# Polymax attention on VectorE: two instructions, add and multiply, replaced by one scalar_tensor_tensor

## The chip, the cores and the metric

The kernel runs on all 8 cores of one Trainium2 chip. Every core executes the same program on its own data: a pair of cores shares one of the four sequences, and each core of a pair owns 16 of the 32 query tiles of 128 rows. There is no traffic between cores. The time is the device time of the slowest core, in microseconds (us).

## The reference

One pre-norm layer over x of shape (4, 4096, 1024), in float32, with 16 heads of 64. In place of softmax the attention uses a polynomial, and masked scores count as zero after it:

```python
def polymax(x):                      # X_INT=-100, Y_INT=1, POWER=2, DIVISOR=1000
    lin  = where((x >= -100) & (x <= 0), -0.01 * x + 1, 0)
    poly = where(x > 0, x ** 2 + 1, 0)
    return (poly + lin) / 1000
...
att = polymax(where(causal, q @ k.T / 8, -inf))
x = x + (att @ v) @ W_proj                       # on layernorm(x)
x = x + gelu((layernorm(x) @ U1) @ V1 + b1) @ U2 @ V2 + b2
```

For a score s between -100 and anything positive, 1000 * polymax(s) = 1 - 0.01 s + r (r + 0.01) with r = max(s, 0). The kernel computes the term r (r + 0.01) tile by tile; the linear term 1 - 0.01 s needs no elementwise work on tiles that are wholly visible, since its sum over keys is a running product of k and v, kept in `msnap` and `prefsnap`.

## The kernel before, in words

The program is written engine by engine: `b.op` appends an instruction to an engine's queue and has it raise that engine's counter, and `b.wait` appends a wait for a counter to the queue, so each engine works through its queue strictly in order. The order in which the Python emits is the order of the work.

The stages are: LayerNorm of x; the K, V and Q projections (lines 616 to 663); attention on the first 2048 keys (`half` 0); the K and V projections of the other 2048 keys (lines 918 to 950); attention on those (`half` 1); the output projection (line 1047); the second LayerNorm and the low-rank FFN.

`emit_attention(half)` runs over four query chunks c of 512 columns and, within each, over 8 pairs p of heads. Such a (c, p) block goes through key tiles of 128 keys: 8 masked ones for c = 0, 8 full ones and 8 masked ones for c = 1, 16 full ones for c = 2 and 3, all in half 0; 8 masked for c = 2, and 8 full and 8 masked for c = 3, in half 1. A tile holds 128 keys by 2 heads by N queries; N is 512 in a full tile, and 512, 512, 384, 384, 256, 256, 128, 128 in the masked ones of a block. So there are 48 blocks and 640 tiles: 384 full, 256 masked, and by size 448 of 1024 elements in each partition (2 x 512) and 64 each of 768, 512 and 256.

A tile idx passes through three engines:

- TensorE: two QK matmuls (line 735) into a pair of PSUM banks. `emit_qk(idx + 3)` stands in its queue ahead of `emit_av(idx)`.
- ScalarE: `relu` of the scores into `eb` (line 756), and on masked tiles also 1 - 0.01 s of the diagonal 128 columns into `zb` (line 761).
- VectorE: `eb + 0.01` into `ab2` (line 770), then `ab2 * eb` into `gb` (line 777); on masked tiles `zb` times the mask (line 783) and `gb` times the mask (line 788), over 128 of the columns.
- TensorE: two AV matmuls (line 810) with `gb`, and on masked tiles two more with the masked `zb` (line 818); the first tile of a block also adds the `msnap` products (line 836).

Buffers `eb` and `gb` and the score banks are rings of three tiles (`sb = idx % 3`), `ab2` one of two. `s_rel` tells that ScalarE has read a score bank, `e_rel` that VectorE has finished with the `eb` slot, `g_rel` that TensorE has finished with the `gb` slot. At the end of a block VectorE copies the result out of PSUM (lines 883 to 895), and TensorE starts the next block's QK only after the last AV.

On VectorE the multiplication of line 777 waits for VectorE's own counter (`b.wait("vector", "V", acnt)`): it reads what line 770 has just written.

Of the kernel before, what the change touches and what calls it, by code (L numbers as in the profile page):

```python
# [11 lines left out]
ALU = mybir.AluOpType  # L12
# [112 lines left out]
def view(pool, byte_off, dtype, shape):  # L125
    esz = mybir.dt.size(dtype)
    assert byte_off % 32 == 0 and byte_off % esz == 0
    n = prod(shape[1:])
    ap = pool.bitcast(dtype).ap()[0:shape[0], byte_off // esz: byte_off // esz + n]
    if len(shape) > 2:  # L130
        names = [f"a{i}" for i in range(len(shape) - 1)]
        spec = "p (" + " ".join(names) + ") -> p " + " ".join(names)
        ap = ap.rearrange(spec, **{names[i]: shape[i + 1] for i in range(len(shape) - 1)})
    return ap


def build_program(upto="full", dumps=()):
# [27 lines left out]
    with contextlib.ExitStack() as stack:  # L165
# [19 lines left out]
        b = Build(nc)  # L185
# [8 lines left out]
        def tfence():  # L194
# [31 lines left out]
        eb = view(poolD, 0, BF16, [128, 6, 512])  # L226
# [11 lines left out]
        ab2 = [view(poolD, 14336, BF16, [128, 2, 512]),  # L238
               view(poolD, 16384, BF16, [128, 2, 512])]
# [24 lines left out]
        def bank(i, lo=0, hi=512):  # L264
            return ps[:, i * 512 + lo: i * 512 + hi]
# [140 lines left out]
        for tb in range(8):  # L406
# [28 lines left out]
            for dc in range(DC):  # L435
                if dc + 2 < DC:
# [9 lines left out]
                     inc="T")  # L446
# [21 lines left out]
        for tb in range(8):  # L468
# [26 lines left out]
            for dc in range(DC):  # L495
                if dc + 2 < DC:
# [3 lines left out]
                                 o=lnxh[tb // 4][:, dc, (tb % 4) * 512:(tb % 4 + 1) * 512],  # L500
                                 t=tmp2[dc % 4], n=bank(bkb): e.tensor_add(o, t, n),
                                 inc="V")
# [188 lines left out]
        def emit_attention(half):  # L691
# [6 lines left out]
            for c in range(4):  # L698
# [3 lines left out]
                for p in range(NP):  # L702
# [5 lines left out]
                    if K_ILV and half == 0 and tb2 == 0:  # L708
# [8 lines left out]
                                         inc="V")  # L717
# [21 lines left out]
                    def is_m(idx):  # L739
                        return 8 * c <= kts[idx] <= 8 * c + 7  # L740

                    gcnt, mcnt, pcnt = {}, {}, {}

                    def emit_eg(idx, qkT):
                        ktg = kts[idx]
                        sb = idx % 3
                        masked = is_m(idx)
                        j0 = max(4 * c + 1, ktg // 2 + 1)
                        coloff = (j0 - (4 * c + 1)) * 128
                        N = 512 - coloff  # L750
                        b.wait("scalar", "T", qkT)
                        b.wait("scalar", "V", e_rel[sb])
                        b.wait("scalar", "P", e_relP[sb])
                        b.op("scalar", lambda e, o=eb[:, 2 * sb:2 * sb + 2, 0:N],
                             i=ps8[:, SBK[sb]:SBK[sb] + 2, 0:N]:
                             e.activation(o, i, AF.Relu), inc="S")  # L756
                        if masked:
                            b.wait("scalar", "V", zw_rel[sb])
                            b.op("scalar", lambda e, o=zb[:, sb, :, :],
                                 i=ps8[:, SBK[sb]:SBK[sb] + 2, 0:128]:  # L760
                                 e.activation(o, i, AF.Identity, scale=-0.01,  # L761
                                              bias=consts[:, 1:2]), inc="S")
                        s_rel[sb] = b.cnt["S"]
                        b.wait("vector", "S", s_rel[sb])
                        if idx >= 2:
                            b.wait("vector", "V", gcnt[idx - 2])
                        acnt = b.op("vector",
                                    lambda e, o=ab2[idx % 2][:, :, 0:N],
                                    i=eb[:, 2 * sb:2 * sb + 2, 0:N]:
                                    e.tensor_scalar_add(o, i, 0.01), inc="V")  # L770
                        b.wait("vector", "T", g_rel[sb])
                        b.wait("vector", "V", acnt)
                        gcnt[idx] = b.op("vector",
                                         lambda e, o=gb[:, 2 * sb:2 * sb + 2, 0:N],
                                         a=ab2[idx % 2][:, :, 0:N],
                                         i=eb[:, 2 * sb:2 * sb + 2, 0:N]:
                                         e.tensor_mul(o, a, i), inc="V")  # L777
                        pcnt[idx] = 0
                        if masked:
                            midx = ktg % 2  # L780
                            zw_rel[sb] = b.op("vector", lambda e, o=zmb[:, sb, :, :],
                                              z=zb[:, sb, :, :], m=masksb[:, midx, :, :]:
                                              e.tensor_mul(o, z, m), inc="V")  # L783
                            b.wait("vector", "V", gcnt[idx])
                            mcnt[idx] = b.op("vector",
                                             lambda e, o=gb[:, 2 * sb:2 * sb + 2, 0:128],
                                             m=masksb[:, midx, :, :]:
                                             e.tensor_mul(o, o, m), inc="V")  # L788
                        e_rel[sb] = b.cnt["V"]
# [56 lines left out]
                    for idx in range(nk):  # L846
                        emit_eg(idx, fences[idx])
                        if idx + 3 < nk:
                            fences[idx + 3] = emit_qk(idx + 3)
                        emit_av(idx)  # L850
                        if K_ILV and half == 0 and idx < 8:
                            b.wait("tensor", "V", kcast[hc])
                            if idx == 0:
                                b.wait("tensor", "V", av_free[idle_bk])
                                b.wait("tensor", "S", av_freeS[idle_bk])
                            b.op("tensor", lambda e, o=bank(idle_bk),
                                 l=wkvh[hc % 2][:, idx, :],
                                 r=lnxh[1][:, idx, tb2 * 512:(tb2 + 1) * 512],
                                 st=(idx == 0), sp=(idx == 7):
                                 e.matmul(o, l, r, skip_group_check=True, start=st,  # L860
                                          stop=sp), inc="T")
# [16 lines left out]
                    for i4 in range(4):  # L878
# [3 lines left out]
                        if not chunk_final:  # L882
                            b.op("vector", lambda e, o=dst, s=src: e.tensor_copy(o, s),
                                 inc="V")
                        elif c <= 1:
                            if j == 1:
                                b.op("vector", lambda e, o=dst, s=src: e.tensor_copy(o, s),
                                     inc="V")
# [4 lines left out]
                        else:  # L893
                            b.op("vector", lambda e, o=dst, s=src, pv=prefsnap[:, j, p:p + 1]:
                                 e.scalar_tensor_tensor(o, s, pv, o, ALU.add, ALU.add),
                                 inc="V")
# [218 lines left out]
        for c in range(4):  # L1115
# [32 lines left out]
            for fc in range(32):  # L1148
# [3 lines left out]
                                      i=bank(2 + fc % 2), bb=b1s[:, fc:fc + 1]:  # L1152
# [136 lines left out]
```

How the kernel before makes its waits and increments, by code:

```python
        def wrapped(e, fn=fn, h=h, w=selfw):  # L60
            i = fn(e)
            if w:
                i.wait_op(h, w, "sem-ge")
            i.then_inc(h, 1)
# [3 lines left out]
    def _dma_on(self, queue, dst, src, slot=None):  # L68
        key = f"dma{self.dma_n}"
        self.dma_n += 1
        if not hasattr(self, "dma_slots"):
            self.dma_slots = {}
        if slot is None:
            slot = key
        if slot not in self.dma_slots:
            assert len(self.dma_slots) < self.N_DMA_SEMS, "DMA sem pool exhausted"
            self.dma_slots[slot] = [self.dma_sems[len(self.dma_slots)], 0]
        ent = self.dma_slots[slot]
        ent[1] += 16
        h = ent[0]
        self.sem_handles[key] = h
        self.cnt[key] = ent[1]
        for e_ in self.ENGINES:
            self.last_wait[e_][key] = 0
        self.streams[queue].append(
            lambda e, d=dst, s=src, h=h: e.dma_start(out=d, in_=s).then_inc(h, 16))
        return key
# [7 lines left out]
    def wait(self, eng, sem, val):  # L95
        if not val or val <= 0:
            return
        if sem.startswith("dma"):
            val = self.cnt[sem]
        assert val <= self.cnt[sem], f"{eng} waits future {sem}={val} (now {self.cnt[sem]})"
        if self.last_wait[eng][sem] >= val:
            return
        self.last_wait[eng][sem] = val
        h = self.sem_handles[sem]
        self.streams[eng].append(lambda e, h=h, v=val: e.wait_ge(h, v))
```

## Time and profile before

| | |
|---|---|
| median of 8 runs | 2139.38 us (2132.04 to 2173.7) |
| the profiled execution's own time | 2140.15 us |
| its span on the slowest core (core 7) | 2138.6 us |
| the other cores' spans | 2118.0 to 2137.8 us |
| mean granted TensorE clock, by core | 0.721 to 0.729 |
| busy on core 7: TensorE, VectorE, ScalarE | 1295.6, 1215.0, 760.7 us |
| lines 770 and 777 together on VectorE | 635.4 us in 1280 instructions |

The span runs from the first to the last instruction; 1.55 us of the execution's time lie outside of it. Busy times add up the durations of instructions, and neighbours on one engine can overlap by some tens of ns, so an engine's cost per tile is read from the starts of its instructions and not from their durations. The attention stages lie at about 518 to 1120 us and 1386 to 1650 us of the span.

### The profile page before, as it was taken

To read this page: it belongs to the slowest core of one execution; us is meant where nothing else is said; L and a number is where in the kernel's file an instruction comes from. 1 tells how busy PE (TensorE), PEld (TensorE's weight loads), DVE (VectorE), ACT (ScalarE), POOL (GpSimd) and SP (SyncE) were. 2 spreads that over 40 slices of the span, in tenths; PEclk is the share of its full clock that TensorE was granted. 3 is DMA by queue.
4 is the path that set the end of the run, shared out by engine and by line. 5 is a ranking of instruction groups with operands and counts; after the bars stand their busy time and mean duration, and the time that the engine had idled before them with its cause. 6 is when DMAs were issued, how large, how long until landed. Compare 5 with 4: busy or idle time off the path is not lost.

```text
span 2138.6 us, 23901 instructions; the slowest of 8 cores (2118.0 to 2138.6 us)
## 1 busy us (share of the span) xinstructions
PE 1295.6 (61%) x6880; PEld 469.6 (22%) x6880; DVE 1215.0 (57%) x2811; ACT 760.7 (36%) x1074; POOL 0.2 (0%) x4
## 2 busy tenths in 40 slices
PE   3423286477667676766662837666765461368886
PEld 0001133243222221111111313322221130023332
DVE  4558433245788888888882323488887233344422
ACT  1200000002667777778770000266775000133332
POOL 0000000000000000000000000000000000000000
PEclk8755597798556668777885969855665685578997
DMA  5445201200000000000002020000000444001011
GB/s 162 157 129 185 79 30 49 79 1 1 1 1 1 1 1 1 1 1 1 1 1 79 13 66 1 1 1 1 1 1 16 153 145 120 0 0 40 40 40 40
DMA packets 37408, 87.76 MB, mean 41 GB/s; under 512 B 1953, under 2 KB 7330, under 8 KB 37282
## 3 DMA queue, kind: packets, MB, share of 16 engines
q1 hardware_dynamic: 30562, 75.75, 10.9%
q10 hardware_dynamic: 6720, 10.49, 1.6%
q8 instruction: 60, 0.98, 0.2%
q14 instruction: 66, 0.54, 0.1%
HBM read 77.85 MB, written 8.39 MB: 40 GB/s over the span
## 4 chain that ended last, share of the span: by engine, by line
PE 45%; DVE 27%; issue 12%; DMA 10%; ACT 4%; DVEq 1%; SPq 0%; ACTq 0%
DVE poolD L777 9%; PE ps L810 8%; DVE poolD L770 6%; DMA poolD<-W_attn 6%; PE ps L735 5%; PE ps L1141 3%; PE ps L946 3%; PE ps L636 3%; PE ps L1047 3%; PE ps L931 3%; PE ps L616 3%; PE ps L658 3%; PE ps L1161 3%; ACT poolD L756 2%; DMA poolD<-W_proj 1%
## 5 line engine op out<-in xcount | busy, mean ns | idle before, releaser
L756 ACT ACTIVATE poolD<-ps 128x1024 bf16<-128x1024 f32 (+3 forms) x640 | 560.9, 901 | 882.2 <-PE ps L735 666.2
L810 PE MATMUL ps<-poolD,poolA 128*64 128x512 bf16 (+3 forms) x1280 | 308.6, 467 | 255.1 <-DVE poolD L777 120.1
L777 DVE TENSOR_TENSOR poolD<-poolD 128x1024 bf16<-128x1024 bf16 (+3 forms) x640 | 391.9, 612 | 68.2 <-DVE poolD L770 2.2
L735 PE MATMUL ps<-poolB,poolA 64*128 64x512 bf16 (+3 forms) x1280 | 285.5, 473 | 33.8 <-ACT poolD L761 16.4
L770 DVE TENSOR_SCALAR poolD<-poolD 128x1024 bf16<-128x1024 bf16 (+3 forms) x640 | 243.5, 380 | 44.3 <-ACT poolD L756 23.2
L810 PEld LDWEIGHTS ps<-poolD,poolA 128*64 128x64 bf16 x1280 | 93.8, 119 | 446.1 <-issue 446.1
L1153 ACT ACTIVATE poolC<-ps,sb_b1s 128x512 bf16<-128x512 f32 x128 | 88.0, 688 | 117.7 <-PE ps L1141 76.8
L761 ACT ACTIVATE poolD<-ps,consts 128x256 bf16<-128x256 f32 x256 | 124.3, 485 | 0.0
L735 PEld LDWEIGHTS ps<-poolB,poolA 64*128 64x128 bf16 x1280 | 65.0, 102 | 237.2 <-issue 236.0
L818 PE MATMUL ps<-poolD,poolA 128*64 128x128 bf16 x512 | 86.6, 306 | 0.0
L946 PE MATMUL ps<-poolD,poolC 128*128 128x512 bf16 x256 | 62.9, 402 | 37.5 <-DVE poolD L918 37.5
L616 PE MATMUL ps<-poolC,poolD 128*128 128x512 bf16 x256 | 57.6, 389 | 41.9 <-DVE poolD L595 41.9
L1047 PE MATMUL ps<-poolC,poolD 128*128 128x512 bf16 x256 | 57.9, 391 | 40.4 <-DVE poolD L989 40.4
L1141 PE MATMUL ps<-poolC,poolB 128*128 128x512 bf16 x256 | 78.8, 393 | 5.4 <-DVE poolC L1126 1.5
L931 PE MATMUL ps<-poolC,poolD 128*128 128x512 bf16 x256 | 57.8, 390 | 38.2 <-DVE poolD L918 38.2
L384 ACT ACTIVATE poolD<-ps 1x512 f32<-1x512 f32 x4 | 2.3, 587 | 216.8 <-PE ps L380 216.8
L658 PE MATMUL ps<-poolC,poolD 128*128 128x512 bf16 x256 | 61.2, 392 | 28.0 <-DVE poolD L595 27.2
L1161 PE MATMUL ps<-poolC,poolB 128*128 128x512 bf16 x256 | 76.7, 382 | 1.5 <-ACT poolC L1153 1.3
L378 PE MATMUL ps<-poolD,sb_onescol 128*1 128x512 bf16 x32 | 18.9, 590 | 95.9 <-DVE poolD L375 95.9
L443 PE MATMUL ps<-poolD,sb_onescol 128*1 128x512 bf16 x64 | 33.0, 515 | 70.1 <-DVE poolD L440 69.9
L636 PE MATMUL ps<-poolD,poolC 128*128 128x512 bf16 x256 | 58.1, 392 | 26.7 <-DVE poolD L595 26.7
L788 DVE TENSOR_TENSOR poolD<-poolD,sb_masksb 128x256 bf16<-128x256 bf16 x256 | 72.7, 284 | 0.3 <-DVE poolD L783 0.3
(101 smaller groups left out, 1224.9 us busy)
## 6 DMA issues: line engine op xcount, KB each, us to landing
poolD<-x_t SPq DMA_DIRECT2D x8, 2048.0 KB, 9.9
poolA<-x_t SPq DMA_DIRECT2D x8, 2048.0 KB, 10.2
poolD<-W_attn SPq DMA_DIRECT2D x12, 1024.0 KB, 5.0
poolD<-W_attn SPq DMA_DIRECT2D x16, 512.0 KB, 3.6
poolC<-x_own_t SPq DMA_DIRECT2D x8, 1024.0 KB, 6.1
y<-poolC SPq DMA_DIRECT2D x4, 2048.0 KB, 6.8
poolD<-W_proj SPq DMA_DIRECT2D x8, 512.0 KB, 3.7
poolD<-U ACTq DMA_DIRECT2D x5, 512.0 KB, 4.8
```

The source lines that it names most:

```text
L636: sp=(dc == DC - 1): e.matmul(o, l, r, skip_group_check=True, start=st, stop=sp), inc="T")
L658: e.matmul(o, l, r, skip_group_check=True, start=st, stop=sp), inc="T")
L735: e.matmul(o, l, r, skip_group_check=True, start=True, stop=True, tile_position=tp),
L756: e.activation(o, i, AF.Relu), inc="S")
L761: e.activation(o, i, AF.Identity, scale=-0.01, bias=consts[:, 1:2]), inc="S")
L770: e.tensor_scalar_add(o, i, 0.01), inc="V")
L777: e.tensor_mul(o, a, i), inc="V")
L810: e.matmul(o, l, r, skip_group_check=True, start=st, stop=True, tile_position=tp),
L946: e.matmul(o, l, r, skip_group_check=True, start=st, stop=sp), inc="T")
L1047: e.matmul(o, l, r, skip_group_check=True, start=st, stop=sp), inc="T")
L1141: e.matmul(o, l, r, skip_group_check=True, start=st, stop=sp), inc="T")
L1161: e.matmul(o, l, r, skip_group_check=True, start=st, stop=sp), inc="T")
```

## The change

The addition into `ab2` and the multiplication that reads it become one `scalar_tensor_tensor`, which computes (eb + 0.01) * eb straight into `gb`. With it go the buffer `ab2`, VectorE's wait for its own addition, and the wait for the multiplication of two tiles earlier. The waits for ScalarE and for the `gb` slot stay.

```diff
                         b.wait("vector", "S", s_rel[sb])
-                        if idx >= 2:
-                            b.wait("vector", "V", gcnt[idx - 2])
-                        acnt = b.op("vector",
-                                    lambda e, o=ab2[idx % 2][:, :, 0:N],
-                                    i=eb[:, 2 * sb:2 * sb + 2, 0:N]:
-                                    e.tensor_scalar_add(o, i, 0.01), inc="V")
                         b.wait("vector", "T", g_rel[sb])
-                        b.wait("vector", "V", acnt)
                         gcnt[idx] = b.op("vector",
                                          lambda e, o=gb[:, 2 * sb:2 * sb + 2, 0:N],
-                                         a=ab2[idx % 2][:, :, 0:N],
                                          i=eb[:, 2 * sb:2 * sb + 2, 0:N]:
-                                         e.tensor_mul(o, a, i), inc="V")
+                                         e.scalar_tensor_tensor(o, i, 0.01, i,
+                                                                ALU.add, ALU.mult),
+                                         inc="V")
```

## Rows read from the trace of the kernel before

**Rows 1.** The page: busy time of the engines, and VectorE in 40 slices (tenths).
```profile
PE 1295.6 (61%) x6880; PEld 469.6 (22%) x6880; DVE 1215.0 (57%) x2811; ACT 760.7 (36%) x1074; POOL 0.2 (0%) x4
DVE  4558433245788888888882323488887233344422
```

**Rows 2.** The two attention stages by windows: stretch, its length, engines' busy us, PEclk, DMA.
```profile
518.00:1120.00 602.00, 409.78 (x2164) 122.38 (x2160) 503.85 (x1268) 445.33 (x574) 0.00 (x0) 0.70 0.00 1
1386.00:1650.00 264.00, 175.80 (x1080) 57.53 (x1076) 221.07 (x670) 185.07 (x304) 0.00 (x0) 0.59 0.00 1
```

**Rows 3.** Waits, 819 to 1120 us: who for whom, us in total, times, longest.
```profile
PE ps L810 <- DVE poolD L777: 84.3, 171, 0.7
DVE poolD L770 <- ACT poolD L756: 11.9, 14, 0.9
```

**Rows 4.** Timeline of VectorE, full tiles: start, duration (us), engine, line, operation.
```profile
962.97 0.42 DVE L770 TENSOR_SCALAR poolD<-poolD 128x1024 bf16<-128x1024 bf16 x1
963.49 0.69 DVE L777 TENSOR_TENSOR poolD<-poolD 128x1024 bf16<-128x1024 bf16 x1
964.10 0.42 DVE L770 TENSOR_SCALAR poolD<-poolD 128x1024 bf16<-128x1024 bf16 x1
...
978.83 0.42 DVE L770 TENSOR_SCALAR poolD<-poolD 128x1024 bf16<-128x1024 bf16 x1
```

**Rows 5.** Timeline of VectorE in one masked block (tiles of 768, 512 and 256).
```profile
613.11 0.35 DVE L770 TENSOR_SCALAR poolD<-poolD 128x768 bf16<-128x768 bf16 x1
613.57 0.56 DVE L777 TENSOR_TENSOR poolD<-poolD 128x768 bf16<-128x768 bf16 x1
614.04 0.28 DVE L783 TENSOR_TENSOR poolD<-poolD,sb_masksb 128x256 bf16<-128x256 bf16 x1
...
614.45 0.35 DVE L770 TENSOR_SCALAR poolD<-poolD 128x768 bf16<-128x768 bf16 x1
...
615.78 0.29 DVE L770 TENSOR_SCALAR poolD<-poolD 128x512 bf16<-128x512 bf16 x1
...
618.05 0.22 DVE L770 TENSOR_SCALAR poolD<-poolD 128x256 bf16<-128x256 bf16 x1
...
618.59 0.28 DVE L783 TENSOR_TENSOR poolD<-poolD,sb_masksb 128x256 bf16<-128x256 bf16 x1
...
618.99 0.22 DVE L770 TENSOR_SCALAR poolD<-poolD 128x256 bf16<-128x256 bf16 x1
```

**Rows 6.** Groups of VectorE by form: count, busy us, mean ns, idle before.
```profile
L777 DVE TENSOR_TENSOR poolD<-poolD 128x1024 bf16<-128x1024 bf16 x448 | 310.3, 693 | 47.6 <-DVE poolD L770 1.4
L770 DVE TENSOR_SCALAR poolD<-poolD 128x1024 bf16<-128x1024 bf16 x448 | 188.5, 421 | 43.6 <-ACT poolD L756 23.2 <-ACT poolD L761 20.0 <-issue 0.2
...
L777 DVE TENSOR_TENSOR poolD<-poolD 128x256 bf16<-128x256 bf16 x64 | 18.7, 292 | 6.8 <-DVE poolD L770 0.4
...
L895 DVE SCALAR_TENSOR_TENSOR poolC<-ps,prefsnap,poolC 128x128 bf16<-128x128 f32 x64 | 18.0, 344 | 10.9 <-PE ps L818 10.9
...
L464 DVE SCALAR_TENSOR_TENSOR poolB<-poolD,poolB 1x512 f32<-1x512 f32 x8 | 5.4, 679 | 12.7 <-ACT poolB L461 12.7
L454 DVE TENSOR_TENSOR poolB<-poolD 1x512 f32<-1x512 f32 x8 | 5.4, 679 | 20.0 <-ACT poolD L452 20.0
```

**Rows 7.** Timeline of VectorE: two groups of four evacuations, each group back to back.
```profile
960.08 0.89 DVE L883 CAST poolC<-ps 128x128 bf16<-128x128 f32 x4 [0.89 <-PE ps L810]
...
1562.56 1.13 DVE L895 SCALAR_TENSOR_TENSOR poolC<-ps,prefsnap,poolC 128x128 bf16<-128x128 f32 x4 [0.68 <-PE ps L818]
```

**Rows 8.** Timeline of ScalarE: masked tiles of 256, then four full tiles together.
```profile
615.96 0.39 ACT L756 ACTIVATE poolD<-ps 128x256 bf16<-128x256 f32 x1 [0.37 <-DVE poolD L788]
616.24 0.47 ACT L761 ACTIVATE poolD<-ps,consts 128x256 bf16<-128x256 f32 x1
...
621.30 3.77 ACT L756 ACTIVATE poolD<-ps 128x1024 bf16<-128x1024 f32 x4 [3.46 <-DVE poolC L892]
```

**Rows 9.** Timeline of TensorE: one AV matmul pair of a masked tile.
```profile
616.01 0.53 PE L810 MATMUL ps<-poolD,poolA 128*64 128x384 bf16 x2 [0.48 <-DVE poolD L788]
```

## The prediction

> **What bounds the kernel now.** I read the page first. Its totals name no bound (TensorE 61% busy, VectorE 57%), but the row of slices does: VectorE stands at 7 to 8 tenths in the slices of the two attention stages and at 2 to 5 in most others [rows 1]. The windows of those two stages, 866 us together, give VectorE 724.9 us, ScalarE 630.4 us, TensorE 585.6 us of busy time [rows 2]. The chain of waits inside them says who is late: in the stretch of full tiles the AV matmuls wait 84.3 us for the multiplication of line 777, while VectorE's addition waits for ScalarE only 14 times, once at the head of each block, 11.9 us in all [rows 3]. So inside a block VectorE is the bound, and ScalarE and TensorE run ahead of it and are held by the rings of three tiles.
>
> Because VectorE is the bound, what matters is the distance between the starts of its instructions. The timeline of full tiles shows it bare: additions at 962.97 and 978.83 with 13 more between them, so 14 tiles in 15.86 us, 1.133 us a tile, of which 0.525 lies between addition and multiplication and 0.61 between multiplication and next addition [rows 4]. The reader should see that these are not the durations (421 and 693 ns, [rows 6]): the next addition starts 80 ns before the multiplication has ended, whereas the multiplication starts some 105 ns after the end of the addition, for whose result it waits.
>
> In a masked block the same is read by size. The two mask products take 614.04 to 614.45 or 618.59 to 618.99, 0.405 us a tile. Two tiles of 768 take 613.11 to 615.78, two of 512 take 615.78 to 618.05, one of 256 takes 618.05 to 618.99 [rows 5]. Less the masks, addition and multiplication together take 0.93 us, 0.73 us and 0.535 us.
>
> **The change part by part.** *Removed: the addition with the wait behind it.* By the starts it holds VectorE for 0.525 us of a 1024 tile [rows 4] and 0.46 us of a 768 tile [rows 5]. The other dropped wait, for the multiplication two tiles back, was over long before and costs nothing now.
>
> *Put in place of the multiplication: one scalar_tensor_tensor, bf16 in and out of SBUF.* The trace has no such row, so its cost has two ends. The multiplication's duration falls from 693 ns at 1024 elements to 292 ns at 256, that is 0.522 ns an element [rows 6]; its spacing of 0.61 us [rows 4] is then 0.075 us plus 0.535 us of elements. The lower end is the same rate: 0.61 us. The upper end is half the rate, 1.044 ns an element: 0.075 + 1.069 = 1.144 us at 1024, 0.877 at 768, 0.61 at 512, 0.342 at 256. Every scalar_tensor_tensor of the trace fits the upper rate: the one with an immediate scalar and both tensors in SBUF (line 464) takes 679 ns for 512 elements, like the tensor_tensor beside it (line 454) [rows 6], and 679 - 512 x 1.044 leaves 144 ns, near the 158 ns that the multiplication leaves by its own rate. But those rows are f32, so they don't settle bf16. I take the upper end, as the rows of the same operation lie there.
>
> The Trainium skill bears on this end: in "Vector Engine (DVE) Microarchitecture Reference", section 2.3, the handler of tensor_tensor carries a parameter that enables the two-source performance mode, and the handler of scalar_tensor_tensor carries none. By that rule the instruction would run at 1.144 us for 1024 elements, by the tensor_tensor row at 0.61; no run here shows it yet.
>
> *Sum, with VectorE as the bound throughout.*
> - 1024 elements: 1.144 - 1.133 = +0.011 us, x 448 = +4.9 us
> - 768: 0.877 - 0.93 = -0.053, x 64 = -3.4 us
> - 512: 0.61 - 0.73 = -0.12, x 64 = -7.7 us
> - 256: 0.342 - 0.535 = -0.193, x 64 = -12.4 us
>
> Together -18.6 us. The fused instruction loses what it saves on large tiles, because the second pass over the elements that it drops was the cheap one, and it gains the fixed part, the wait of 0.105 us and the addition's own overhead, on small ones.
>
> *What hides or limits it.* In the masked tiles that gain, ScalarE needs 0.28 us from relu to linear part plus at most 0.47 us for that part at 256 elements, 0.75 us at most, and idles 0.37 us for VectorE before it [rows 8]; VectorE's new tile is 0.342 + 0.405 = 0.747 us. That is close, but ScalarE enters those tiles up to three tiles ahead. TensorE idles 0.48 us for VectorE before an AV pair there [rows 9], and the tile gives back at most 0.19. If that cover were gone, the 23.5 us of gains would go and +4.9 us stay.
>
> *Waits.* The wait for the gb slot now stands ahead of all of the tile's VectorE work, where the addition went ahead of it. Behind it queue the mask products, and the AV matmuls wait for those. It asks for the AV of three tiles earlier, and that AV begins once its own tile's VectorE work has ended, two whole VectorE tiles (1.5 us at least) before the wait is reached; it costs nothing. At the head and the tail of a block the latency from relu to AV is 0.525 + 0.693 = 1.22 us before and 1.069 + 0.15 = 1.22 us after, so the 48 gaps between blocks stay. No transfer moves: the DMA share is 0.00 in both stages [rows 2].
>
> The profiled execution took 2140.15 us, of which 2138.6 is the span; less 18.6 that is 2121.5 us. The median of the runs shown is 0.8 us lower than this execution, so I predict 2121 us. A difference of 0.3%, about 6 us, is what a measurement of this kernel can tell from none.
>
> **The rivals.**
> - *The bf16 form runs at the multiplication's rate.* For it: operand types and layout are the multiplication's, and that row runs at 0.522 ns. Against it: no row of the operation is that fast. VectorE would need 0.61 us a full tile and ScalarE would be the bound, at 3.77 / 4 = 0.94 us [rows 8]: 384 full tiles x 0.19 = 74 us, and about 0.25 us on each of 256 masked ones, 64 us; about 2000 us. TensorE's 585.6 us over 640 tiles, 0.915 a tile [rows 2], leaves little slack and may hold it at up to 2050.
> - *Slower: the fused instruction has a larger fixed part than the multiplication.* Place: each of the 640 tiles. Four scalar_tensor_tensors of line 895 take 1.13 us in sequence and four casts of the same size 0.89 [rows 7], 60 ns more for each. With 60 ns on each tile the sum is -18.6 + 38.4 = +19.8 us, 2160 us; it decides from 29 ns on. Against it: line 895 reads a column of prefsnap as its scalar, and line 464 with an immediate shows no surplus over line 454 [rows 6]. A related form is that the next instruction cannot overlap: 80 ns x 640 = 51 us less 18.6, 2173 us. But the four of line 895 take 1.13 us where four durations of 344 ns would be 1.38, so this operation does overlap its like [rows 6, 7]. [...]
> - *The small tiles' gain is not turned into time,* since ScalarE or the ring sets the pace there. For it: 0.75 against 0.747 us. Against it: ScalarE's idle time for VectorE. The result is between 2121 and 2145 us, near 2142.
>
> **How the numbers follow.** My forecast has a chance of 0.70, between 2112 and 2130 us (a fixed part 15 ns off moves it by 9.6 us); the fast rate 0.08; the larger fixed part 0.13; no gain 0.09. Leaving out the fast rate (0.08) and most of the larger fixed part, the range is 2110 to 2146 us. Faster by over 0.3%: 0.69 of the forecast's 0.70 plus 0.08, 0.77. Slower by over 0.3%: 0.13 less a little for a small surplus, 0.12. Within: 0.11.
>
> **What the profile after would show.** The fused row of 1024 elements at 1.21 to 1.23 us mean (0.69 would be the fast rate); 1.144 us from start to start in full tiles, where 1.20 would mean the larger fixed part; masked tiles of 768, 512 and 256 at 1.28, 1.015 and 0.75 us; line 777's predecessor wait gone; still about 0.6 to 1.0 us of idle time on VectorE at a block's head, and ScalarE waiting for VectorE inside blocks. VectorE's busy time in lines 770 and 777, 635.4 us, would rise to about 680 us with less elapsed time. If ScalarE becomes the releaser inside masked blocks, the no-gain case is on.

## The result and the profile after

The changed kernel takes 2109.82 us (median of 11 runs) where the kernel before takes 2138.97 (median of 32 in all): ratio 0.9887, 95% interval 0.9869 to 0.9906, faster by 1.1%, some 24 us (20 to 28). The forecast was 18.6 us.

Some executions of both kernels are slower, with a lower granted clock on some of the cores; the medians, 29.15 us apart, include them, the ratio leaves them out, and of the profiled execution (2127.41 us, granted clock 0.714 to 0.721 on cores 4 to 7 and 0.725 to 0.728 on cores 0 to 3) I compare not the span but the lengths of the two attention stages, which hardly differ between cores. These lengths are read from the first and the last QK matmul of each half. The view of one line's instructions on core 0 (count, shortest/median/longest ns, first to last start in us; the shapes behind are counted in a part of the group only), for the kernel before:

```profile
L735 PE MATMUL ps<-poolB,poolA x896: 226/407/632, 512.1 to 1116.2; 64*128 64x512 bf16 x141, 64*128 64x384 bf16 x13, 64*128 64x256 bf16 x13, 64*128 64x128 bf16 x13
L735 PE MATMUL ps<-poolB,poolA x384: 227/393/632, 1363.0 to 1635.2; 64*128 64x512 bf16 x96, 64*128 64x384 bf16 x32, 64*128 64x256 bf16 x32, 64*128 64x128 bf16 x32
```

and for the kernel after:

```profile
L735 PE MATMUL ps<-poolB,poolA x896: 279/393/632, 513.8 to 1106.1; 64*128 64x512 bf16 x141, 64*128 64x384 bf16 x13, 64*128 64x256 bf16 x13, 64*128 64x128 bf16 x13
L735 PE MATMUL ps<-poolB,poolA x384: 278/393/632, 1354.6 to 1614.0; 64*128 64x512 bf16 x96, 64*128 64x384 bf16 x32, 64*128 64x256 bf16 x32, 64*128 64x128 bf16 x32
```

Half 0 fell from 604.1 to 592.3 us and half 1 from 272.2 to 259.4. Over the eight cores the sum of both has its median at 876.3 us before and 852.0 after, 24.3 us less, and no core is further than 1.1 us from its median. So the whole gain that the ratio shows lies in attention.

The page of the kernel after, totals and VectorE by slices, against [rows 1]: VectorE is busier and the kernel shorter.

```profile
PE 1316.5 (62%) x6880; PEld 474.9 (22%) x6880; DVE 1257.8 (59%) x2171; ACT 760.7 (36%) x1074; POOL 0.2 (0%) x4
DVE  4558433245889999999982323589995233334422
```

VectorE's groups by form, where [rows 6] had additions and multiplications (busy us, then mean ns; the busy time counts the overlap of neighbours of one group once, so it is less than count times mean):

```profile
L769 DVE SCALAR_TENSOR_TENSOR poolD<-poolD 128x1024 bf16<-128x1024 bf16 x448 | 516.3, 1219 | 43.9 <-ACT poolD L756 23.3 <-ACT poolD L761 20.0 <-issue 0.2
...
L769 DVE SCALAR_TENSOR_TENSOR poolD<-poolD 128x768 bf16<-128x768 bf16 x64 | 60.8, 951 | 0.2 <-ACT poolD L761 0.2
L769 DVE SCALAR_TENSOR_TENSOR poolD<-poolD 128x512 bf16<-128x512 bf16 x64 | 43.7, 683 | 0.2 <-issue 0.2
...
L769 DVE SCALAR_TENSOR_TENSOR poolD<-poolD 128x256 bf16<-128x256 bf16 x64 | 26.7, 417 | 0.5 <-PE ps L812 0.2 <-issue 0.2
```

From 417 ns at 256 elements to 1219 at 1024 is 1.044 ns an element, twice the 0.522 of the multiplication that it replaces: the fused instruction runs at half the multiplication's rate on bf16. The idle time ahead of it is that of block heads, as it was ahead of the addition (43.9 against 43.6 us); the 47.6 us ahead of the multiplication are gone.

The starts on VectorE's timeline, full tiles first and then the small tiles of a masked block, against [rows 4, 5]:

```profile
968.83 17.12 DVE L769 SCALAR_TENSOR_TENSOR poolD<-poolD 128x1024 bf16<-128x1024 bf16 x15 [0.86 <-ACT poolD L756]
```
```profile
626.72 0.95 DVE L769 SCALAR_TENSOR_TENSOR poolD<-poolD 128x768 bf16<-128x768 bf16 x1
627.59 0.28 DVE L777 TENSOR_TENSOR poolD<-poolD,sb_masksb 128x256 bf16<-128x256 bf16 x1
...
629.27 0.68 DVE L769 SCALAR_TENSOR_TENSOR poolD<-poolD 128x512 bf16<-128x512 bf16 x1
...
631.28 0.41 DVE L769 SCALAR_TENSOR_TENSOR poolD<-poolD 128x256 bf16<-128x256 bf16 x1
...
632.02 0.42 DVE L769 SCALAR_TENSOR_TENSOR poolD<-poolD 128x256 bf16<-128x256 bf16 x1
```

Fifteen full tiles run in 17.12 us; less the last one's 1.22 that is 14 spacings of 1.136 us, where the pair took 1.133. A masked tile of 768 takes 1.275 us (two in 626.72 to 629.27) where it took 1.335, one of 512 takes 1.005 instead of 1.135, one of 256 takes 0.74 instead of 0.94.

Waits after, 819 to 1106 us, against [rows 3]: VectorE still sets the pace, and ScalarE is still waited for only at the 14 block heads.

```profile
PE ps L804 <- DVE poolD L769: 79.3, 162, 0.7
...
DVE poolD L769 <- ACT poolD L756: 12.0, 14, 0.9
```

### The profile page after: what moved, and what is told of

It is laid out like the page before. It is cut to its first block, busy times and chain, and to the rows that moved or that the text cites. A ratio compares the mean times of both kernels' runs of the same rounds, so it can differ in the third digit from the quotient of the medians.

```text
span 2125.8 us, 22621 instructions; the slowest of 8 cores (2099.0 to 2125.8 us)
## 1 busy us (share of the span) xinstructions
PE 1316.5 (62%) x6880; PEld 474.9 (22%) x6880; DVE 1257.8 (59%) x2171; ACT 760.7 (36%) x1074; POOL 0.2 (0%) x4
## 4 chain that ended last, share of the span: by engine, by line
PE 41%; DVE 27%; issue 16%; DMA 10%; ACT 4%; DVEq 1%; SPq 0%; ACTq 0%
DVE poolD L769 15%; DMA poolD<-W_attn 6%; PE ps L804 5%; PE ps L1135 3%; PE ps L735 3%; PE ps L1155 3%; PE ps L1041 3%; PE ps L940 3%; PE ps L636 3%; PE ps L658 3%; PE ps L616 3%; PE ps L925 3%; ACT poolD L756 2%; DVE poolD L782 2%; DMA poolD<-W_proj 1%
## 5 line engine op out<-in xcount | busy, mean ns | idle before, releaser
L769 DVE SCALAR_TENSOR_TENSOR poolD<-poolD 128x1024 bf16<-128x1024 bf16 (+3 forms) x640 | 647.5, 1059 | 44.8 <-ACT poolD L756 23.3
L1135 PE MATMUL ps<-poolC,poolB 128*128 128x512 bf16 x256 | 89.4, 440 | 2.1 <-DVE poolC L1120 1.5
L1155 PE MATMUL ps<-poolC,poolB 128*128 128x512 bf16 x256 | 88.5, 433 | 1.4 <-ACT poolC L1147 1.4
L782 DVE TENSOR_TENSOR poolD<-poolD,sb_masksb 128x256 bf16<-128x256 bf16 x256 | 72.5, 283 | 1.0 <-DVE poolD L777 1.0
L777 DVE TENSOR_TENSOR poolD<-poolD,sb_masksb 128x256 bf16<-128x256 bf16 x256 | 72.5, 283 | 0.0
```

What stands on the lines that cost most here:

```text
L769: e.scalar_tensor_tensor(o, i, 0.01, i, ALU.add, ALU.mult),
L1135: e.matmul(o, l, r, skip_group_check=True, start=st, stop=sp), inc="T")
L1155: e.matmul(o, l, r, skip_group_check=True, start=st, stop=sp), inc="T")
```

## The experiments

The column "stages" is the sum of both attention stages, first to last QK matmul, median of the eight cores; ratios are against the kernel before, timed on the same chip. A ratio rests on 2 to 11 executions of the run, its stages on one profiled execution. The diffs below are shortened, with `...` or a comment for what is left out; those of the runs with the addition one tile ahead are written against the kernel before.

| run | ratio (95% interval) | stages, us |
|---|---|---|
| before | 1 | 876.3 |
| after (the change) | 0.9887 (0.9869 to 0.9906) | 852.0 |
| fused on small tiles only | 0.9913 (0.9882 to 0.9944) | 853.8 |
| fused on 1024 tiles only | 1.0001 (0.997 to 1.0032) | 877.2 |
| change + one small instruction | 1.0102 (1.007 to 1.0135) | 903.3 |
| multiplication left out | 0.9176 (0.9156 to 0.9196) | 703.5 |
| addition one tile ahead | 1.0246 (1.0197 to 1.0296) | 928.3 |
| the same, four eb slots | 1.0202 (1.018 to 1.0224) | 922.6 |
| the same, QK ahead of AV | 0.9742 (0.9704 to 0.978) | 819.0 |
| QK ahead of AV, three eb slots | 1.0032 (1.0019 to 1.0044) | 885.2 |
| mixed by block | 0.971 (0.9676 to 0.9744) | 816.7 |

### Where the gain sits: small tiles alone, large tiles alone

```diff
+ if N < 512:      # second run: N == 512
+     gcnt[idx] = b.op("vector", ... scalar_tensor_tensor(o, i, 0.01, i, ALU.add, ALU.mult))
+ else:
      acnt = ... tensor_scalar_add ...
      gcnt[idx] = ... tensor_mul ...
```

> The fused instruction only on the 192 tiles of 768, 512 and 256 elements; the 448 tiles of 1024 keep addition and multiplication. Theory (VectorE's start-to-start spacing is the time of a tile, and the fused instruction costs 0.068 us plus 1.042 ns an element): the whole gain of the change and a trifle more, about -25 us against the kernel before, ratio 0.988; the two attention stages together, from first to last QK matmul, 25 us shorter than 876 us. Rival (each tile gains the same, 24 us / 640 = 37 ns, because a wait and an instruction go): -7 us, ratio 0.997.

> The fused instruction only on the 448 tiles of 1024 elements; the small ones keep two instructions. Theory: 1.135 us in place of 1.133 on each, +1 us, no change that can be told, ratio 0.999 to 1.002. Rival (each tile gains 37 ns): -17 us, ratio 0.992.

On the 192 small tiles the fusion shortens the stages by 22.5 us, on the 448 large ones it lengthens them by 0.9. An equal gain on each tile would have given 7 and 17. So the gain comes from the small tiles, and the large ones break even. The first is 2.5 us short of its expectation, and both together make 21.6 where the change makes 24.3; those 2.7 us I did not follow up. By the starts, 1.4 us of the 2.5 are a few full tiles that take some 0.35 us longer in the first run (the median spacing of full tiles stays at 1.133 us, their mean is 1.142 against 1.138 before); what held them is not shown.

### Does every ns on VectorE count?

```diff
  gcnt[idx] = ... scalar_tensor_tensor ...
+ tcnt[idx] = b.op("vector", lambda e, o=ab2[idx % 2][:, :, 0:32], i=eb[:, 2*sb:2*sb+2, 0:32]:
+                  e.tensor_scalar_add(o, i, 0.01), inc="V")
+ # ahead of it: a wait for the same instruction of two tiles earlier
```

> The changed kernel with one more VectorE instruction in each tile, an addition over 64 elements into a buffer that nothing reads. Theory (VectorE is the bound in every tile): its own spacing, 0.07 to 0.10 us, on all 640 tiles, +45 to +64 us over the changed kernel, +20 to +40 us over the kernel before. Rival (ScalarE or the rings set the pace of the small masked tiles): the 192 small tiles would not show it, +31 to +45 us over the changed kernel, and their spacing would stay at 1.27, 1.00 and 0.74 us.

VectorE's timeline of this run, in full tiles:

```profile
960.07 0.17 DVE L777 TENSOR_SCALAR poolD<-poolD 128x64 bf16<-128x64 bf16 x1
960.15 1.21 DVE L769 SCALAR_TENSOR_TENSOR poolD<-poolD 128x1024 bf16<-128x1024 bf16 x1
961.29 0.17 DVE L777 TENSOR_SCALAR poolD<-poolD 128x64 bf16<-128x64 bf16 x1
961.37 1.22 DVE L769 SCALAR_TENSOR_TENSOR poolD<-poolD 128x1024 bf16<-128x1024 bf16 x1
```

The tile goes from 1.136 to 1.22 us. The stages are 51.3 us longer than after the change, 80 ns on each of 640 tiles, the spacing of the extra instruction itself (0.08 us; its duration is 0.17). Had the 192 small tiles hidden it, 36 us would have come. By the starts, on all cores, the tiles of 768, 512 and 256 take 80, 83 and 72 ns longer. VectorE is the bound in all tiles, against the rival.

The other direction, with the work left out (this run was made after the run with the addition one tile ahead, which follows below and which theory B takes its numbers from):

```diff
- e.scalar_tensor_tensor(o, i, 0.01, i, ALU.add, ALU.mult)
+ e.tensor_scalar_add(o, i, 0.01)
```

> The changed kernel with the multiplication left out: one addition (eb + 0.01 into gb) stands in place of the fused instruction, so the term r (r + 0.01) is computed wrongly as r + 0.01 and VectorE needs 0.34 us a full tile. It shows what the attention would take if VectorE cost next to nothing. Theory A (ScalarE is next, 0.94 us a full tile and about 1.05, 0.85 and 0.65 on the small masked ones): 75 us less on full tiles and some 65 on masked ones, ratio 0.93 to 0.95 against the kernel before. Theory B, from the run with the addition one tile ahead (TensorE at the lower clock level, about 0.53 + 0.57 us for QK and AV of a full tile, is next): 1.10 to 1.15 us stays on full tiles, only masked tiles gain, ratio 0.965 to 0.985, and the granted clock in the stretch of full tiles falls from 0.78 to about 0.55.

ScalarE's timeline of this run shows what comes next, one block of 16 full tiles:

```profile
886.02 14.77 ACT L756 ACTIVATE poolD<-ps 128x1024 bf16<-128x1024 f32 x16 [2.11 <-DVE poolC L875]
```

and VectorE's, waiting for it in each tile:

```profile
888.07 0.43 DVE L769 TENSOR_SCALAR poolD<-poolD 128x1024 bf16<-128x1024 bf16 x1 [0.49 <-ACT poolD L756]
888.98 0.43 DVE L769 TENSOR_SCALAR poolD<-poolD 128x1024 bf16<-128x1024 bf16 x1 [0.48 <-ACT poolD L756]
```

The stages fall by 173 us, to 703.5. Theory A's mechanism holds, and theory B's is out: VectorE waits for ScalarE tile by tile, and relus follow each other in (14.77 - 1.03) / 15 = 0.916 us, where 0.94 was taken. Its size does not hold: the ratio of 0.9176 lies below its 0.93 to 0.95. By the starts, full tiles give 65 us (mean 1.138 to 0.962; 75 were expected), masked ones within a block 83, and 26 come from the steps between blocks, which the theory did not count. Between 1.136 and 0.916 us a full tile there is room, which neither kernel uses.

### The wait alone, without fusing

The forecast put 0.105 us of waiting and 0.08 us of lost overlap into each tile of the kernel before. If that is right, hiding the wait should pay more than the fusion does.

```diff
- acnt = tensor_scalar_add(ab2[idx % 2], eb[idx]);  wait V acnt;  tensor_mul(gb[idx], ...)
+ # per tile idx: relu and tensor_scalar_add of idx + 1 into ab2[(idx + 1) % 3],
+ # then tensor_mul of idx (its addition is one tile old)
```

> Two instructions as before, but the addition is issued one tile ahead of its multiplication, into a ring of three buffers, so the wait for the own result is covered by the multiplication of the tile before. Theory (the wait costs 0.185 us a tile, and VectorE is the bound): 0.34 + 0.61 = 0.95 us a full tile, near ScalarE's 0.94, so 384 x 0.18 = 70 us less and up to 0.18 us on each of 256 masked tiles, 46 us; minus something at the 48 block heads, where the first multiplication now stands behind the second tile's relu: -60 to -115 us, ratio 0.946 to 0.972. Rival (the gap between addition and multiplication is not the wait but a cost of the instructions, or another engine sets the pace as soon as VectorE is faster): about 0 to -20 us, with the gap still 0.1 us in the trace, or with ScalarE or TensorE as releaser of most tiles.

Both expectations failed. From addition to multiplication it is 0.34 us in 98% of all full-size tiles, so the gap was the wait, against the rival; from multiplication to the next addition it is 0.60 us where nothing else is waited for, but that is one case in ten, and the kernel became 2.5% slower, against the theory. From VectorE's timeline:

```profile
951.63 0.43 DVE L771 TENSOR_SCALAR poolD<-poolD 128x1024 bf16<-128x1024 bf16 x1 [0.39 <-ACT poolD L757]
...
951.98 0.68 DVE L785 TENSOR_TENSOR poolD<-poolD 128x1024 bf16<-128x1024 bf16 x1
...
952.74 0.43 DVE L771 TENSOR_SCALAR poolD<-poolD 128x1024 bf16<-128x1024 bf16 x1
...
953.08 0.68 DVE L785 TENSOR_TENSOR poolD<-poolD 128x1024 bf16<-128x1024 bf16 x1
```

The chain of waits of this run (start, us, what) names the loops:

```profile
951.98 0.70 DVE poolD L785
...
952.76 1.03 ACT poolD L757
...
953.95 0.44 DVE poolD L771
...
954.48 0.70 DVE poolD L785
...
955.32 0.64 PE ps L818 x2
955.96 0.58 PE ps L736 x2
...
956.68 1.03 ACT poolD L757
```

L785 is the multiplication, L771 the addition, L757 relu, L818 AV, L736 QK. (The 0.53 us from the addition at 953.95 to the multiplication is one of the exceptions.) The first step goes from a multiplication straight to a relu: it freed the eb slot, which the addition in front of it had made it hold a tile longer. The last steps go from a multiplication through AV to the QK that stands behind that AV in TensorE's queue, and from there to relu. With the addition ahead, each loop spans one tile less than before. The next runs take the loops away, one at a time and both.

```diff
+ eb4 = [eb[:, 0:2, :], eb[:, 2:4, :], eb[:, 4:6, :], view(poolD, 22528, BF16, [128, 2, 512])]
+ # eb4[idx % 4] and e_rel[idx % 4] in place of three slots
```

> The kernel with the addition one tile ahead, and the ring of eb (ScalarE's output) widened from three slots to four. Theory A (putting the addition of the next tile in front of the multiplication held an eb slot one tile longer, so that the ring of three acted as one of two, and that took away the gain): VectorE's 0.95 us a full tile is reached, masked tiles gain up to 0.18 us, attention stages 60 to 110 us shorter than the 876 us before, ratio 0.95 to 0.97. Theory B (TensorE at its lower clock level set the pace there): full tiles at 1.10 to 1.15 us, ratio 0.985 to 1.005, granted clock about 0.53 in full tiles.

Neither theory gave the number: 922.6 us, 5.7 less than with three slots, above both ranges. The granted clock fell as B said (0.56 at 820 to 1060 us), but it is not the whole of it: in a stretch with a granted clock of 1.00 (948 to 953 us), that is 2.4 GHz, where the QK pair takes 0.39 us, the additions are 1.11 us apart all the same. From the timeline of this run:

```profile
950.39 0.43 DVE L773 TENSOR_SCALAR poolD<-poolD 128x1024 bf16<-128x1024 bf16 x1
...
950.85 0.39 PE L738 MATMUL ps<-poolB,poolA 64*128 64x512 bf16 x2
...
951.50 0.43 DVE L773 TENSOR_SCALAR poolD<-poolD 128x1024 bf16<-128x1024 bf16 x1
```

The fourth slot alone is not enough; the next run also moves QK.

```diff
  emit_e(idx + 1)                      # relu and addition of the next tile
+ fences[idx + 4] = emit_qk(idx + 4)   # its score bank is free after relu of idx + 1
  emit_g(idx)
- fences[idx + 3] = emit_qk(idx + 3)
  emit_av(idx)
```

> The kernel with the addition one tile ahead and four eb slots, and the QK matmuls one tile earlier too: QK of tile idx + 4 now stands in TensorE's queue ahead of AV of tile idx, where it stood behind it. Theory A (in the two runs before, a loop set the pace: end of the multiplication of idx, AV of idx, QK of idx + 4 behind it in TensorE's queue, relu, addition of idx + 4, multiplication of idx + 3, about 3.3 us for three tiles, 1.1 us a tile; with QK ahead of AV the loop no longer goes through that AV): full tiles at VectorE's 0.95 to 1.0 us, attention stages 50 to 110 us shorter than 876 us, ratio 0.95 to 0.98. Theory B (TensorE's lower clock level sets the pace by itself): 1.10 us or more on full tiles, stages between 850 and 920 us, ratio 0.99 to 1.02.

> The same with three eb slots. Theory A: the eb slot now closes a loop of its own: end of the multiplication of idx, relu of idx + 3, addition of idx + 3, multiplication of idx + 2, about 2.3 us for two tiles, 1.15 us a tile, so no gain on full tiles against the kernel before, stages 860 to 910 us, ratio 0.99 to 1.02. Theory C (the place of QK alone was the cause, the slots don't matter): the same as with four slots, ratio 0.95 to 0.98.

With four slots and QK ahead of AV the stages take 819.0 us and the kernel 0.9742 of before, better than the change. Its VectorE timeline:

```profile
904.89 0.42 DVE L773 TENSOR_SCALAR poolD<-poolD 128x1024 bf16<-128x1024 bf16 x1
...
905.23 0.69 DVE L787 TENSOR_TENSOR poolD<-poolD 128x1024 bf16<-128x1024 bf16 x1
...
905.83 0.42 DVE L773 TENSOR_SCALAR poolD<-poolD 128x1024 bf16<-128x1024 bf16 x1
...
906.16 0.69 DVE L787 TENSOR_TENSOR poolD<-poolD 128x1024 bf16<-128x1024 bf16 x1
```

The addition now holds VectorE for 0.34 us instead of 0.525, and the tile takes 0.94 us here; over all full tiles that is the median, while the mean is 1.02. With QK ahead but three slots it is 885.2 us: each loop alone is enough to undo the gain, and theory C falls.

The windows of 820 to 1050 us on core 0 (the number ahead of the last two is the granted clock), before, with the addition ahead, and with QK ahead of AV as well:

```profile
820.00:1050.00 230.00, 160.31 (x722) 43.72 (x720) 192.86 (x398) 175.68 (x178) 0.00 (x0) 0.77 0.00 1
```
```profile
820.00:1050.00 230.00, 180.61 (x666) 42.27 (x666) 173.87 (x366) 163.07 (x162) 0.00 (x0) 0.55 0.00 1
```
```profile
820.00:1050.00 230.00, 174.96 (x800) 47.22 (x800) 202.07 (x442) 187.11 (x198) 0.00 (x0) 0.78 0.00 1
```

With the addition ahead TensorE ran mostly at 1.2 GHz, which lengthens the loop through it (an AV pair takes 0.64 us, and 0.41 in the stretch at 2.4 GHz above). Whether the loop brought the clock down is not settled by these runs. They do show that a slower pace is enough for it: the changed kernel with the extra instruction, where no loop was touched and VectorE alone takes 80 ns more a tile, has 0.59 in the same window of core 0, and at that clock its tile is still no longer than VectorE needs (1.22 us). With QK ahead of AV the pace and the clock came back together.

Last, the two ways together:

```diff
+ fused = is_m(0)     # blocks that begin with a masked tile: scalar_tensor_tensor
+                     # the other 32 blocks: addition one tile ahead
```

> The best of both: the 16 blocks that begin with a masked tile (c = 0 in half 0, c = 2 in half 1) use the fused instruction, the 32 blocks that begin with a full tile use two instructions with the addition one tile ahead, four eb slots and QK ahead of AV. Theory: a block of masked tiles takes 12.0 us in the changed kernel and 12.4 us with the addition ahead (which waits at the block's head for the second tile's two ScalarE instructions), so 16 x 0.4 = 6 us less than the run with the addition ahead everywhere: attention stages about 813 us, ratio 0.970 to 0.974 against the kernel before. Rival (the QK order or the wider ring already gives the masked blocks what the fusion gives): no difference, 819 us.

816.7 us lies between theory (813) and rival (819): half 0 gained 1.9 us, half 1 nothing (258.6 against 258.7). The ratio's interval overlaps that of the run before, so I claim no difference between them; both beat the two kernels of this study.

## Why the prediction was right, point by point

- **The bound.** VectorE inside the blocks: right, by the extra instruction (80 ns on every tile) and by the left-out work.
- **The rate.** I took the half rate because the operation's rows lay there, and expected a duration of 1.21 to 1.23 us at 1024 elements; it is 1.219 us. The double-rate rival is out. From the rows alone the choice was a guess that came true: line 454's tensor_tensor takes the same 679 ns in f32, and in bf16 that operation runs at 0.522 ns an element, so f32 rows could not tell the two rates apart. The Trainium skill ("Vector Engine (DVE) Microarchitecture Reference", section 2.3: no two-source performance mode in the handler of scalar_tensor_tensor) agrees with this trace's 1.044 ns an element.
- **The number.** The forecast of 18.6 us is a quarter less than the 24.3 us that attention gave back, and the median of 2109.82 us lies just beneath the forecast's range (2110 to 2146). (By the ratio, 24 us off the 2139.38 that the forecast started from, it would be 2115, inside the range.) The mechanism and the sign of the total were right; the size was short by one term, named below.
- **The sum.** From the starts of all tiles on cores 0 to 3, mean spacing before and after:

| tiles | forecast, us | measured, us |
|---|---|---|
| 448 of 1024 | +4.9 | -0.3 (368 full at 1.138 and 1.139, 64 masked at 1.558 and 1.548) |
| 64 of 768 | -3.4 | -4.3 (1.350 to 1.283) |
| 64 of 512 | -7.7 | -8.1 (1.142 to 1.016) |
| 64 of 256 | -12.4 | -12.0 (0.945 to 0.760 within a block, the same 0.19 at its end) |
| together | -18.6 | -24.6 before rounding (stages: -24.3) |

- **The term that was off** is the fused instruction's fixed part. I carried over the multiplication's 0.075 us; the spacing of 1.136 us less 1024 x 1.044 = 1.069 leaves 0.067. The durations say the same: 1219 - 1069 leaves 150 ns, where the multiplication left 158. 8 ns less on each of 640 tiles is 5.1 us, nearly all of the missing 5.7. By the medians of the spacings (1.135, 1.273, 1.006 and 0.740 us), the masked sizes too are 7 to 9 ns below the forecast. The sign of the large tiles' term hung on those 8 ns.
- **The larger fixed part,** my slower rival, is out by the same number. Of its related form: the next instruction starts before the fused one has ended (626.72 + 0.95 is later than 627.59) by 0.08 us. The Trainium skill ("VectorE: DVE Perf Modes", The DRAIN you can't avoid) lets a next instruction start only once the pipe is empty, except that one "that is not held starts earlier"; this trace shows the exception.
- **No gain on small tiles** is out by the run on small tiles alone.
- **Heads and tails, waits, transfers** cost nothing, as said: idle time at the heads is 43.9 us against 43.6, and from the last full tile of a block to the first of the next it is 3.81 us in both kernels.
- **VectorE's busy time** was to rise from 635.4 to about 680 us. The durations of the fused instruction do add up to 677 us, but the profile's busy time, 647.5 us for the four groups, counts their overlap once.

What I did not see is that the kernel has little slack in its loops: the wait was worth 0.185 us a tile, as worked out, but only with another eb slot and another place for QK can it be had.

## What to carry to other kernels

On a bound VectorE, compare spacings from start to start, not durations: a scalar_tensor_tensor on bf16 costs 0.067 us plus 1.044 ns an element here, and replaces a fast tensor_scalar and a tensor_tensor that waits for it at no gain at 1024 elements a partition and at a good third less at 256. Before moving an instruction one tile ahead to hide a wait, follow each loop that it closes through buffers and through the queue of the other engines; a loop that spans one tile less can cost more than the wait.

## What the hardware showed that I had not expected

The addition over 64 elements costs VectorE 0.08 us although its duration is 0.17: neighbours without a wait between them overlap by some 0.08 us, whether the first takes 0.17 us, 0.69 (the multiplication) or 1.22 (the fused instruction); for the shortest that is half of it. And hiding a wait on the bound engine made the whole kernel 2.5% slower, with the granted clock of TensorE in full tiles at 0.55 in place of 0.77, until QK was put ahead of AV (0.78).
